# Edge counts as a product of their own in single pass form, and split operands in the first product of an expert layer

## The chip, the cores and the metric

The kernel runs on one core of a Trainium2 chip. The metric is the device time of one execution in microseconds. A core has TensorE (matrix products), VectorE, ScalarE, GpSimd and SyncE, each with its own instruction stream in order, and DMA engines that move data between memories. Engines wait for each other on semaphores. fp32 products are issued as two instructions each; the type fp32r (R32 in the code) is a rounded form that takes one instruction, and full precision is kept by splitting an operand in an upper part (the rounded value) and a lower part (the rest).

## The reference

Two layers over a graph of 3125 nodes with 256 features and 50,000 edges. What matters here:

```python
# first graph layer: messages of 64 features, 4 heads
exp_scores = exp(scores - max)
sum_exp = segment_sum(exp_scores, dst)
outs = [segment_sum(messages * (exp_scores / sum_exp[dst])[:, hd:hd+1], dst) for hd in range(4)]

# first expert layer, 8 experts, each token to its best 2
logits = xf @ gate_w + gate_b
top2_vals, top2_idx = top_k(softmax(logits), 2)
h = gelu(xf @ W1[e] + b1[e])          # 256 -> 512
y = h @ W2[e] + b2[e]                 # 512 -> 256
out = sum over the two experts of weight * y

# second graph layer: mean over incoming edges
deg = segment_sum(ones, dst)
agg = segment_sum(x[src], dst) / max(deg, 1)
```

The degrees of the nodes, which the second layer divides by, are counted in the first layer's edge sums.

## The kernel before

The program is one long sequence of stages, written engine by engine; all order is by hand.

**The edge sums (stage 3).** The 50,000 edges, sorted by destination, lie in 400 chunks of 128. They are worked off in NCG = 40 passes of 10 chunks, in PR = 5 pairs. The edges of a pair fall in a window of W = 48 nodes. For a pass n:
- VectorE (`one_hots`, L3018) writes for each edge the one-hot of its destination in the window, in column block MH = 4 of `ohx`.
- GpSimd (`weigh_hots`, L1052) multiplies it by the exponentials of heads 0 to 2 in two instructions, then sets a column of ones behind the messages (`ones_column`, L1038) and, in the first 25 passes, adds a tile of the input to z (L1063). ScalarE (L2178) does head 3 in ten small instructions.
- TensorE (L1556) multiplies the messages with the column of ones (65 rows) by the five blocks of 48: 240 columns, fp32, two products for each pair. The block of the unweighted one-hots gives the counts in its last row.
- VectorE (`add_windows`, L3034) adds each window of 65 x 5 x 48 at its place in `acc`; each addition waits for the one before.

`ohx` and the messages have two buffers; VectorE issues the one-hots of pass n+1 ahead of the additions of pass n.

**The first expert layer.** The tokens, sorted by expert, form NUN = 32 units of 256 tokens, each with one expert. For a unit u:
- GpSimd fetches its rows of x (L1095), TensorE turns them (`x_turn`, L1631), VectorE copies them from PSUM to `xtT` (`x_keep`, L3260).
- SyncE loads the expert's W1 (512 KB) into one of three buffers of `e1` (`up_weights`, L871). The load of unit u+3 is issued behind the two stores of unit u (L879), which wait for its results.
- For each of MT = 4 blocks f of 128 hidden features: TensorE makes `expert_up(u, f)` (L1642, fp32, 256 columns, two products), ScalarE the gelu (L2211), TensorE `expert_down(u, f)` (L1653, fp32). TensorE issues up of the next step ahead of down of this one, and x_turn(u+2) at f = 2.
- VectorE adds the bias (`keep_y`, L3272) and SyncE stores. VectorE's order in the loop is keep_y(u-1), x_keep(u+2), and at u = 8 to 14 a piece of preparation for the next layer (L3279 to L3291 and the splits at L2594, L2595). In the first turn of SyncE's loop 26 small and large loads for the next layer are issued behind the load of unit 3 (L863).

`hi_lo_products` (L631) makes a product of split operands from three fp32r instructions: upper by upper, upper by lower, lower by upper. It is used in most other stages.

Of the kernel before, what the change touches and what calls it, by code (L numbers as in the profile page):

```python
# [18 lines left out]
F32 = mybir.dt.float32  # L19
R32 = mybir.dt.float32r  # L20
# [5 lines left out]
P = 128  # L26
# [18 lines left out]
W = 48  # L45
# [113 lines left out]
def build(nc, ctx, a, out):  # L159
# [140 lines left out]
    msg = sb("msg", [P, 2, CG, MW], F32, s3)  # L300
    ohx = sb("ohx", [P, 2, CG, MH + 1, W], F32, s3)
    ohs = sb("ohs", [P, WS], F32, s3)
# [66 lines left out]
    hn2 = sb("hn2", [TP, GT, D], F32, s6m)  # L369
    xtT = sb("xtT", [P, 2, H, UT], F32, s6m)  # L370
    be6 = sb("be6", [P, NE, D], F32, s6m)
# [21 lines left out]
    oha = sb("oha", [TP, 2, 2, GT, 2 * NUN], R32, s6m)  # L393
    cc = sb("cc", [TP, NT, NE], F32, s6m)
    s6m.close()
    s6 = ExitStack()
# [35 lines left out]
    aw = sb("aw", [P, H, D], F32, s7k)  # L432
    awx = [sb(f"awx{k}", [P, H, D], R32, s7k) for k in range(2)]
    s7k.close()
    kv = sb("kv", [TP, GT * 2 * H, P + 4], F32, s7)
# [5 lines left out]
    s7k = ExitStack()  # L441
    kvq = sb("kvq", [TP, GT, 2, D], F32, s7k)
    s7k.close()
    mw = [sb(f"mw{k}", [P, 2 * H, D], R32, s7) for k in range(2)]
# [145 lines left out]
    for new, old, value in (("e_ld0", "wq_ld", 128), ("e_ld1", "bo_ld", 128), ("e_ld2", "wvo_ld", 128), ("e_ld3", "sm_ld", 320),  # L590
                            ("row2_st0", "row_st", 32 * NG + 16), ("row2_st1", "x_ld", 32), ("x_ld1", "p7_ld", 0), ("x_ld2", "p9_ld", 0),
                            ("x_ld3", "f_ld0", 0), ("x_ld4", "f_ld1", 0), ("be6_ld", "w_ld", 48),
                            ("z_add", "tn_T", NL), ("z_ve", "cx_ps", NL), ("z_nr", "cx_go", NL), ("hot_w", "bq_ps", NL), ("b1_go", "bq_ev", NL),
                            ("tab_go", "tn_go", NL), ("acc1_0", "ta_go", NL), ("xg_ld0", "gat0", 16 * GC * NCG), ("xg_ld1", "gat1", 16 * GC * NCG),
                            ("xg_T", "n_T", 3 * NG * NL), ("xg_up", "n_hi", 3 * NG * NL),
                            ("yo_go", "m_add", 3 * NG * NL), ("uw_ld0", "msg_st0", 16 * NCG), ("uw_ld1", "msg_st1", 16 * NCG), ("uw_ld2", "msg_ld0", 8 * NCG), ("yo_st0", "w1_ld", 48), ("yo_st1", "w2_ld", 64),
                            ("rw5", "gat0", 16 * GC * NCG + 16 * NUN), ("rw6", "gat1", 16 * GC * NCG + 16 * NUN), ("ch_used", "bc_ps", NL * NG),
                            ("cg_ld0", "rw0", 0), ("cg_ld1", "rw1", 0), ("cg_ld2", "rw2", 0), ("cg_ld3", "rw3", 0),
                            ("cg_used", "d_add", GT * NL * NG), ("tr_hi", "q_hi", 3 * NG * NL)):
        s[new], past[new] = s[old], value  # L600
# [110 lines left out]
    def _(sp):  # L711
# [155 lines left out]
        def up_weights(u):  # L867

            if u >= 3:
                sp.wait_ge(s["up_ps"], F_MOE + (u - 2) * MT)  # L870
            sp.dma_start(e1[:, u % 3, :, :], a["L0_ffn_W1"][expert_of(experts, u)].rearrange("o (h p) n -> p (o h) n", p=P)  # L871
                         ).then_inc(s[f"uw_ld{u % 3}"], 16)
# [64 lines left out]
    def _(pool):  # L937
# [106 lines left out]
        def weigh_hots(n):  # L1044

            if n == 0:
                pool.wait_ge(s["act_go"], 1 + MH)
            pool.wait_ge(s["oh_ready"], n + 1)
            for at in (slice(0, 4), slice(4, CG)):
                cols = slice(n * CG + at.start, n * CG + at.stop)  # L1050
                k = at.stop - at.start
                nc.gpsimd.tensor_tensor(ohx[:, n % 2, at, 0:MH - 1, :], ohx[:, n % 2, at, MH:MH + 1, :].to_broadcast([P, k, MH - 1, W]),  # L1052
                                        ex[:, cols, 0:MH - 1].unsqueeze(3).to_broadcast([P, k, MH - 1, W]),
                                        ALU.mult).then_inc(s["wm_ready"], 1)

        for n in range(NCG):
            weigh_hots(n)
            if n >= 2:
                ones_column(n)
            if n == 0:  # L1060
                pool.wait_ge(s["xin_ld"], 32)
            if n < NT:
                me(nc.gpsimd.tensor_tensor(z[:, n, :], z[:, n, :], xin[:, n, :], ALU.add))  # L1063
        me(nc.gpsimd.memset(tri[:, :, :], 1.0))
# [104 lines left out]
    def _(pe):  # L1169
# [377 lines left out]
        for n in range(NCG):  # L1547
            b = n % 2
            pe.wait_ge(s["msg_one"], n + 1)
            for q in range(PR):  # L1550
                pe.wait_ge(s["wm_ready"], 2 * n + (1 if q < 2 else 2))
                pe.wait_ge(s["ax_ready"], n * PR + q + 1)
                if n:
                    pe.wait_ge(s["win_used"], (n - 1) * PR + q + 1)
                for c in (2 * q, 2 * q + 1):
                    last = nc.tensor.matmul(wbank[q][0:MF + 1, 0:(MH + 1) * W], msg[:, b, c, 0:MF + 1],  # L1556
                                            ohx[:, b, c].rearrange("p k w -> p (k w)"), start=c == 2 * q, stop=c == 2 * q + 1)
                last.then_inc(s["win_ps"], 1)
# [76 lines left out]
        def expert_up(u, f):  # L1635

            F = F_MOE + u * MT + f
            pe.wait_ge(s["xg_up"], past["xg_up"] + u + 1)
            pe.wait_ge(s[f"uw_ld{u % 3}"], past[f"uw_ld{u % 3}"] + 16 * (u // 3 + 1))
            pe.wait_ge(s["gf_done"], F + 1)  # L1640
            for k in range(H):
                last = nc.tensor.matmul(pb[:, f % 2, 0:UT],  # L1642
                                        e1[:, u % 3, k, f * P:(f + 1) * P], xtT[:, u % 2, k, :], start=k == 0, stop=k == H - 1)
            last.then_inc(s["up_ps"], 1)
# [301 lines left out]
    def _(act):  # L1946
# [226 lines left out]
        for n in range(NCG):  # L2173
            b = n % 2
            act.wait_ge(s["oh_ready"], n + 1)
            for q in range(PR):
                for c in (2 * q, 2 * q + 1):
                    last = nc.scalar.mul(ohx[:, b, c, MH - 1, :], ohx[:, b, c, MH, :], ex[:, n * CG + c, MH - 1:MH])  # L2178
                last.then_inc(s["ax_ready"], 1)
# [19 lines left out]
        for g in range(NG):  # L2199
            act.wait_ge(s["dve_go"], 9 + RR + g)  # L2200
            for j in range(GT):
                nc.scalar.mul(oha[:, g % 2, :, j, :], oha[:, g % 2, :, j, :].bitcast(F32), idf[:, g * GT + j:g * GT + j + 1]).then_inc(s["hot_w"], 1)
        nc.scalar.activation(hid[:, 0, 0:1], ones[:, 0:1], ACT.Gelu).then_inc(s["act_go"], 1)
        act.wait_ge(s["act_go"], ACT_GO + 1)
        act.wait_ge(s["b1_go"], past["b1_go"] + 1)
        for u in range(NUN):
            for f in range(MT):
                F = F_MOE + u * MT + f
                act.wait_ge(s["up_ps"], F + 1)
                act.wait_ge(s["act_used"], F + 1)  # L2210
                nc.scalar.activation(hid[:, f, :], pb[:, f % 2, 0:UT], ACT.Gelu, bias=b1u[:, u, f:f + 1]).then_inc(s["gf_done"], 1)  # L2211
        act.nop().then_inc(s["f_hi"], NUN * MT)
        act.wait_ge(s["yo_go"], past["yo_go"] + 2 * NUN)
# [165 lines left out]
    def _(dve):  # L2379
# [636 lines left out]
        def one_hots(n):  # L3016

            nc.vector.tensor_tensor(ohx[:, n % 2, :, MH, :], iota[:, 0:W].unsqueeze(1).to_broadcast([P, CG, W]),  # L3018
                                    relT[:, n * CG:(n + 1) * CG].unsqueeze(2).to_broadcast([P, CG, W]),
# [8 lines left out]
        def add_windows(n, starts):  # L3028

            for q, at in enumerate(starts):  # L3030
                dve.wait_ge(s["win_ps"], n * PR + q + 1)
                if n * PR + q:
                    dve.wait_ge(s["win_used"], n * PR + q)
                nc.vector.tensor_tensor(acc[:, :, bass.ds(at, W)], acc[:, :, bass.ds(at, W)],  # L3034
                                        wbank[q][0:MF + 1, 0:(MH + 1) * W].rearrange("p (k n) -> p k n", k=MH + 1),
                                        ALU.add).then_inc(s["win_used"], 1)

        one_hots(0)
        for n in range(NCG):
# [6 lines left out]
            add_windows(n, window_starts(n))  # L3046
        dve.wait_ge(s["win_used"], NPR)
        dve.wait_ge(s["act_go"], 2 + MH)
        dve.nop().then_inc(s["win_used"], PR)
# [196 lines left out]
        dve.wait_ge(s["tab_go"], past["tab_go"] + 1)  # L3246
        nc.vector.tensor_copy(tabi[:, :], pg[:, 0, 0:2 * NUN]).then_inc(s["tab_go"], 1)
        for f in range(MT):
            me.link(dve, nc.vector.tensor_tensor(hits, own, b1r[:, :, f].unsqueeze(1).to_broadcast(by_unit), ALU.mult))
# [5 lines left out]
        def x_keep(u):  # L3255

            dve.wait_ge(s["xg_T"], past["xg_T"] + u + 1)
            if u >= 2:
                dve.wait_ge(s["up_ps"], F_MOE + (u - 1) * MT)
            nc.vector.tensor_copy(xtT[:, u % 2], pt[:, u % 2, :].rearrange("p (k n) -> p k n", k=H)).then_inc(s["xg_up"], 1)  # L3260

# [36 lines left out]

        x_keep(0)
        x_keep(1)  # L3300
        dve.wait_ge(s["pe_go"], 12 + RR)
# [3 lines left out]
        for u in range(NUN):  # L3305
            if u:
                keep_y(u - 1)
            if u + 2 < NUN:
                x_keep(u + 2)
            if u == 8:  # L3310
# [401 lines left out]
```

## Time and profile before

| | us |
|---|---|
| median of 3 runs | 2693.89 (2690.0 to 2704.63) |
| the profiled execution | 2691.82 |
| its span in the trace | 2690.1 |
| edge sums | about 1259 to 1443 |
| loop over the expert units | 1541.5 to 1779.2 |

In rows that list instructions in order of time the columns are: start, duration, engine, line, operation, output <- input, shapes, count, and in brackets how long the engine had been idle and what ended that. PE is TensorE, PEld its weight loads, DVE VectorE, ACT ScalarE, POOL GpSimd, SPq the queue of SyncE. The granted clock of TensorE is given as a share of 2.4 GHz.

### The profile page before, as it was taken

How to read it: one execution, taken by the hardware profiler on the slowest of the kernel's cores; microseconds unless marked ns; L12 is line 12 of the kernel's file. 1: busy time of each engine (PE TensorE's matmuls, PEld its weight loads, DVE VectorE, ACT ScalarE, POOL GpSimd, SP SyncE). 2: the span in 40 equal slices, each digit the busy share in tenths (PEclk: the TensorE clock that was granted, in tenths of full speed). 3: DMA queues.
4: the chain of work that ended last, by engine and by line, in shares of the span. 5: the costliest groups of instructions: out<-in, count | busy, mean ns of one | idle time of the engine just before them, and what ended most of it. 6: DMA issues, size and time to landing. Idle time of an engine off the chain costs nothing. (4 is left out here: it accounts for less than half of the span.)

```text
span 2690.1 us, 46341 instructions
## 1 busy us (share of the span) xinstructions
PE 2428.9 (90%) x16026; PEld 2242.4 (83%) x16026; DVE 1738.7 (65%) x4274; ACT 1352.7 (50%) x2913; POOL 1244.5 (46%) x1402
## 2 busy tenths in 40 slices
PE   6888999899989998997999699966888999999998
PEld 6778998899988997996668688855778799998998
DVE  6666877678767776764656523246876677677565
ACT  4334656466545655555553322233234366665687
POOL 1323454245524551564876232245767377776000
PEclk9789999999999999999997599977989699999899
DMA  5211112111121111124223354536666076775011
GB/s 119 67 39 40 40 43 76 32 40 43 43 66 38 44 46 48 45 58 101 79 84 91 106 169 144 144 111 179 199 194 193 17 215 200 219 220 177 24 36 32
DMA packets 150284, 259.75 MB, mean 97 GB/s; under 512 B 35713, under 2 KB 95884, under 8 KB 149926
## 3 DMA queue, kind: packets, MB, share of 16 engines
q0 software_dynamic: 49632, 145.61, 19.9%
q1 hardware_dynamic: 100422, 111.17, 13.7%
q8 instruction: 132, 2.16, 0.3%
q14 instruction: 98, 0.80, 0.1%
HBM read 219.88 MB, written 36.82 MB: 95 GB/s over the span
## 5 line engine op out<-in xcount | busy, mean ns | idle before, releaser
L974 POOL DMA_INDIRECT gat<-table,srcT x400 | 414.2, 1036 | 352.9 <-DVE m L2820 230.3
L1129 POOL DMA_INDIRECT x_rows<-table,srcT x392 | 402.2, 1026 | 176.9 <-issue 122.7
L631 PE MATMUL pa<-w,act 128*125 128x256 f32 x2400 | 359.2, 288 | 13.0 <-DVE act L2579 12.8
L631 PE MATMUL pb<-hT,w 128*128 128x378 f32 (+1 forms) x1920 | 337.2, 312 | 1.8 <-DVE hT L2655 1.0
L631 PEld LDWEIGHTS pa<-w,act 128*125 128x125 f32 x2400 | 314.6, 187 | 17.7 <-DVE act L2579 17.6
L631 PEld LDWEIGHTS pb<-hT,w 128*128 128x128 f32 x1920 | 287.7, 190 | 4.1 <-DVE hT L2655 1.8
L2278 ACT ACTIVATE gf<-pb,bne 128x378 f32<-128x378 f32 (+1 forms) x320 | 193.9, 606 | 154.9 <-PE pb L631 143.5
L2579 DVE TENSOR_TENSOR act<-gf,act 128x378 fp32r<-128x378 f32 (+1 forms) x320 | 153.8, 483 | 106.7 <-ACT act L1996 104.9
L1993 ACT ACTIVATE gf<-pb,b1s 128x378 f32<-128x378 f32 (+1 forms) x320 | 165.6, 517 | 108.2 <-PE pb L631 98.3
L631 PE MATMUL pb<-xT,fw 128*128 128x378 f32 (+1 forms) x960 | 158.8, 316 | 0.0
L1996 ACT ACTIVATE act<-gf 128x378 fp32r<-128x378 f32 (+1 forms) x320 | 149.8, 468 | 10.1
L2211 ACT ACTIVATE hid<-pb,b1u 128x256 f32<-128x256 f32 x128 | 60.6, 473 | 185.0 <-PE pb L1642 185.0
L631 PE MATMUL pb<-act,fw 128*128 128x378 f32 (+1 forms) x960 | 153.4, 309 | 0.0
L3555 DVE TENSOR_TENSOR act<-gf,act 128x378 fp32r<-128x378 f32 (+1 forms) x180 | 87.8, 488 | 101.3 <-ACT act L2282 100.6
L1095 POOL DMA_INDIRECT xtok<-table,tabi x64 | 61.4, 959 | 190.2 <-PE pt L1631 139.7
L631 PEld LDWEIGHTS pb<-xT,fw 128*128 128x128 f32 x960 | 146.1, 196 | 1.4 <-issue 1.3
L631 PEld LDWEIGHTS pb<-act,fw 128*128 128x128 f32 x960 | 141.7, 190 | 0.0
L2178 ACT ACTIVATE ohx<-ohx,ex 128x48 f32<-128x48 f32 x400 | 94.4, 321 | 84.3 <-DVE ohx L3018 84.3
L1642 PE MATMUL pb<-xtT,e 128*128 128x256 f32 x512 | 132.9, 382 | 2.3 <-DVE xtT L3260 2.3
L1730 PE MATMUL pg<-x_rows,oh 128*125 128x256 f32 x632 | 105.1, 294 | 27.4 <-DMA x_rows<-table,srcT 17.8
L1052 POOL TENSOR_TENSOR ohx<-ohx,ex 128x576 f32<-128x576 f32 x80 | 110.0, 1396 | 35.5 <-DVE ohx L3018 35.2
L1556 PE MATMUL pa<-ohx,msg 128*65 128x240 f32 x480 | 106.5, 372 | 15.7 <-POOL ohx L1052 12.6
(513 smaller groups left out, 5602.5 us busy)
## 6 DMA issues: line engine op xcount, KB each, us to landing
e<-in_L_ffn_W_dram SPq DMA_DIRECT2D x40, 512.0 KB, 4.1
spill<-m SPq DMA_DIRECT2D x80, 170.0 KB, 1.9
msg<-spill SPq DMA_DIRECT2D x40, 340.0 KB, 2.9
yslots<-yo SPq DMA_DIRECT2D x64, 128.0 KB, 2.0
fraw<-in_L_ffn_W_dram SPq DMA_DIRECT2D x32, 256.0 KB
w1r<-in_L_mix_W_dram SPq DMA_DIRECT2D x7, 1024.0 KB, 5.0
gat<-table,srcT POOLq DMA_INDIRECT x400
x_rows<-table,srcT POOLq DMA_INDIRECT x392, 3.7
```

What stands on the lines that cost most here:

```text
L631: mm = nc.tensor.matmul(ps, lhs(l), rhs(r), start=first and n == 0, stop=last and n == 2)
L974: pool.indirect_dma_start(out=gat[:, i % 2, c, :], out_offset=None, in_=table0, in_offset=bass.IndirectOffsetOnAxis(ap=srcT[:, i * GC + c: ...
L1052: nc.gpsimd.tensor_tensor(ohx[:, n % 2, at, 0:MH - 1, :], ohx[:, n % 2, at, MH:MH + 1, :].to_broadcast([P, k, MH - 1, W]), ex[:, cols, 0:M ...
L1129: pool.indirect_dma_start(out=x_rows[:, n % UB, c, :].bitcast(F32), out_offset=None, in_=table1, in_offset=bass.IndirectOffsetOnAxis(ap=sr ...
L1556: last = nc.tensor.matmul(wbank[q][0:MF + 1, 0:(MH + 1) * W], msg[:, b, c, 0:MF + 1], ohx[:, b, c].rearrange("p k w -> p (k w)"), start=c ...
L1642: last = nc.tensor.matmul(pb[:, f % 2, 0:UT], e1[:, u % 3, k, f * P:(f + 1) * P], xtT[:, u % 2, k, :], start=k == 0, stop=k == H - 1)
L1730: last = nc.tensor.matmul(to, oh1[:, n % UB, c, :], x_rows[:, n % UB, c, k * D:(k + 1) * D], start=c == 0 and k == 0, stop=c == UG - 1 and ...
L1993: nc.scalar.activation(gf[:, f % 2, 0:n], pb[:, f % 2, 0:n], func, bias=bias, scale=scale).then_inc(s["gf_done"], 1)
L1996: nc.scalar.activation(act_[0][:, f % 4, 0:n], gf[:, f % 2, 0:n], ACT.Copy).then_inc(s["f_hi"], 1)
L2178: last = nc.scalar.mul(ohx[:, b, c, MH - 1, :], ohx[:, b, c, MH, :], ex[:, n * CG + c, MH - 1:MH])
L2278: nc.scalar.activation(gf[:, f % 2, 0:n], pb[:, f % 2, 0:n], func, bias=bias, scale=scale).then_inc(s["gf_done"], 1)
L2579: nc.vector.tensor_tensor(act_[1][:, f % 4, 0:n], gf[:, f % 2, 0:n], act_[0][:, f % 4, 0:n], ALU.subtract).then_inc(s["f_lo"], 1)
```

## The change

The edge sums: the one-hots get a tile of their own, `ohd`, in fp32r. The five blocks of `ohx` become four. The counts are made by two fp32r products a pass (the even and the odd chunks of all five pairs, 240 columns) of a tile of ones by the one-hots, into a PSUM bank of their own, and VectorE adds them to `acc` in an addition of 48 columns behind each window's. The additions of GpSimd to z are spread over the 40 passes.

The expert layer: W1 of a unit is split into `e1s[0]` (ScalarE, `up_upper`, behind the gelu of the same f two units ahead) and `e1s[1]` (VectorE, `up_lower`, behind keep_y(u-1) and ahead of x_keep(u+2)); `xtT` is split by x_keep in two operations. `expert_up` uses hi_lo_products. The loads of e1 wait for the lower parts in place of the products. `expert_down` stays as it is.

```diff
-    ohx = sb("ohx", [P, 2, CG, MH + 1, W], F32, s3)
+    ohx = sb("ohx", [P, 2, CG, MH, W], F32, s3)
+    ohd = sb("ohd", [P, 2, CG, W], R32, s3)
+    ohd_one = sb("ohd_one", [P, MF + 1], R32, s3)
...
         def up_weights(u):
             if u >= 3:
-                sp.wait_ge(s["up_ps"], F_MOE + (u - 2) * MT)
+                sp.wait_ge(s["us_lo"], past["us_lo"] + (u - 2) * MT)
...
-            if n < NT:
-                me(nc.gpsimd.tensor_tensor(z[:, n, :], z[:, n, :], xin[:, n, :], ALU.add))
+            for t in range(n * NT // NCG, (n + 1) * NT // NCG):
+                me(nc.gpsimd.tensor_tensor(z[:, t, :], z[:, t, :], xin[:, t, :], ALU.add))
...
+                if q == 0:
+                    if n >= 2:
+                        pe.wait_ge(s["deg_used"], past["deg_used"] + (n - 1) * PR)
+                    hots = ohd[:, b].rearrange("p (q k) w -> p q k w", k=2)
+                    for k in range(2):
+                        nc.tensor.matmul(pt[0:MF + 1, b, 0:PR * W].rearrange("p (q w) -> p q w", q=PR), ohd_one[:, :], hots[:, :, k, :],
+                                         start=k == 0, stop=k == 1)
                 for c in (2 * q, 2 * q + 1):
-                    last = nc.tensor.matmul(wbank[q][0:MF + 1, 0:(MH + 1) * W], msg[:, b, c, 0:MF + 1],
+                    last = nc.tensor.matmul(wbank[q][0:MF + 1, 0:MH * W], msg[:, b, c, 0:MF + 1],
...
         def expert_up(u, f):
-            pe.wait_ge(s[f"uw_ld{u % 3}"], past[f"uw_ld{u % 3}"] + 16 * (u // 3 + 1))
+            pe.wait_ge(s["us_lo"], past["us_lo"] + u * MT + f + 1)
             for k in range(H):
-                last = nc.tensor.matmul(pb[:, f % 2, 0:UT],
-                                        e1[:, u % 3, k, f * P:(f + 1) * P], xtT[:, u % 2, k, :], start=k == 0, stop=k == H - 1)
+                last = hi_lo_products(pb[:, f % 2, 0:UT], lambda l: e1s[l][:, u % 2, k, f * P:(f + 1) * P],
+                                      lambda r: xtT[r][:, u % 2, k, :], k == 0, k == H - 1)
...
+        def up_upper(u, f):
+            if f == 0:
+                act.wait_ge(s[f"uw_ld{u % 3}"], past[f"uw_ld{u % 3}"] + 16 * (u // 3 + 1))
+            at = slice(f * P, (f + 1) * P)
+            nc.scalar.activation(e1s[0][:, u % 2, :, at], e1[:, u % 3, :, at], ACT.Copy).then_inc(s["us_hi"], 1)
+        for u in range(2):
+            for f in range(MT):
+                up_upper(u, f)
...
                 nc.scalar.activation(hid[:, f, :], pb[:, f % 2, 0:UT], ACT.Gelu, bias=b1u[:, u, f:f + 1]).then_inc(s["gf_done"], 1)
+                if u + 2 < NUN:
+                    up_upper(u + 2, f)
...
+                degrees = acc[:, MH:MH + 1, bass.ds(at, W)].rearrange("p o n -> p (o n)")
+                nc.vector.tensor_tensor(degrees, degrees, pt[0:MF + 1, n % 2, q * W:(q + 1) * W], ALU.add).then_inc(s["deg_used"], 1)
...
+        def up_lower(u, f):
+            dve.wait_ge(s["us_hi"], past["us_hi"] + u * MT + f + 1)
+            at = slice(f * P, (f + 1) * P)
+            nc.vector.tensor_tensor(e1s[1][:, u % 2, :, at], e1[:, u % 3, :, at], e1s[0][:, u % 2, :, at], ALU.subtract).then_inc(s["us_lo"], 1)
+        for f in range(MT):
+            up_lower(0, f)
...
-            nc.vector.tensor_copy(xtT[:, u % 2], pt[:, u % 2, :].rearrange("p (k n) -> p k n", k=H)).then_inc(s["xg_up"], 1)
+            turned = pt[:, u % 2, :].rearrange("p (k n) -> p k n", k=H)
+            me.link(dve, nc.vector.tensor_copy(xtT[0][:, u % 2], turned))
+            nc.vector.tensor_tensor(xtT[1][:, u % 2], turned, xtT[0][:, u % 2], ALU.subtract).then_inc(s["xg_up"], 1)
...
         x_keep(0)
+        for f in range(MT):
+            up_lower(1, f)
         x_keep(1)
...
             if u:
                 keep_y(u - 1)
             if u + 2 < NUN:
+                for f in range(MT):
+                    up_lower(u + 2, f)
                 x_keep(u + 2)
```

## Rows read from the trace of the kernel before

**Rows 1.** The page, part 1: busy time, share of the span, instructions
```profile
PE 2428.9 (90%) x16026; PEld 2242.4 (83%) x16026; DVE 1738.7 (65%) x4274; ACT 1352.7 (50%) x2913; POOL 1244.5 (46%) x1402
```

**Rows 2.** Stretch of the expert loop: busy time by engine, clock, DMA
```profile
1541.50:1779.20 237.70, 236.93 (x1150) 207.79 (x1150) 56.73 (x119) 60.59 (x128) 61.59 (x60) 0.99 0.47 142
```

**Rows 3.** Waits in the expert loop: total us, times, longest
```profile
ACT hid L2211 <- PE pb L1642: 173.8, 127, 2.7
```

**Rows 4.** Order of time, end of one expert unit, all engines
```profile
1661.59 1.03 PE L1642 MATMUL pb<-xtT,e 128*128 128x256 f32 x4
...
1662.45 0.59 PE L1653 MATMUL pa<-e,hid 128*128 x2
1662.65 0.47 ACT L2211 ACTIVATE hid<-pb,b1u 128x256 f32<-128x256 f32 x1 [1.69 <-PE pb L1642]
...
1663.19 0.42 DVE L3272 TENSOR_TENSOR yo<-pa,be 128x256 f32<-128x256 f32 x1 [1.58 <-PE pa L1653]
1663.31 1.03 PE L1642 MATMUL pb<-xtT,e 128*128 128x256 f32 x4
1663.62 0.42 DVE L3272 TENSOR_TENSOR yo<-pg,be 128x256 f32<-128x256 f32 x1
...
1664.62 0.39 SPq L871 DMA_DIRECT2D e<-in_L_ffn_W_dram  x1
```

**Rows 5.** Order of time, two passes of the edge sums
```profile
1327.18 2.65 PE L1556 MATMUL pa<-ohx,msg 128*65 128x240 f32 x12
1327.34 0.40 DVE L3034 TENSOR_TENSOR acc<-acc,pb 65x240 f32 x1 [0.41 <-PE pb L1556]
1327.66 0.65 DVE L3018 TENSOR_TENSOR ohx<-iota,relT 128x480 f32<-128x480 f32 x1
...
1328.39 2.75 POOL L1052 TENSOR_TENSOR ohx<-ohx,ex 128x576 f32<-128x576 f32 x2 [0.60 <-DVE ohx L3018]
...
1329.66 1.78 PE L1556 MATMUL pb<-ohx,msg 128*65 128x240 f32 x8
...
1331.28 2.61 PE L1556 MATMUL pa<-ohx,msg 128*65 128x240 f32 x12
...
1335.49 2.65 PE L1556 MATMUL pa<-ohx,msg 128*65 128x240 f32 x12
```

**Rows 6.** Order of time in another stage: fp32r products, a copy by ScalarE
```profile
1241.25 0.88 PE L631 MATMUL pa<-w,act 128*125 128x256 f32 x6
...
1241.95 0.41 ACT L1996 ACTIVATE act<-gf 128x252 fp32r<-128x252 f32 x1
1241.97 0.86 PE L631 MATMUL pb<-hT,w 128*128 128x252 f32 x6
```

**Rows 7.** VectorE's groups in the expert loop: busy us, mean ns, idle before
```profile
L2595 DVE TENSOR_TENSOR kvw<-qw,kvw 128x256 fp32r<-128x256 f32 x4 | 1.7, 424 | 0.1
...
L3280 DVE TENSOR_SCALAR kvm<-kvm 125x16 f32<-125x16 f32 x1 | 0.2, 181 | 0.0
```

**Rows 8.** Single lines of VectorE: ns min/median/max, first and last start
```profile
L3260 DVE COPY xtT<-pt x32: 681/691/692, 1540.8 to 1763.8; 128x512 f32<-128x512 f32 x32
...
L3290 DVE TENSOR_TENSOR qw<-qw,wmean x2: 691/692/692, 1618.4 to 1625.9; 128x512 f32<-128x512 f32 x2
```

**Rows 9.** The loads of e1 (L871, 32 of them), from issue to landing
```profile
DMA to landing us min/median/max: 3.6/3.9/6.5
```

**Rows 10.** TensorE behind two gaps, and the clock behind the first
```profile
1868.74 0.76 PE L1730 MATMUL pg<-x_rows,oh 128*125 128x256 f32 x2 [4.92 <-DMA x_rows<-table,srcT]
1870.09 0.79 PE L1730 MATMUL pg<-x_rows,oh 128*125 128x256 f32 x2 [0.58 <-DMA x_rows<-table,srcT]
...
1249.40 1.69 PE L631 MATMUL pa<-w,act 128*125 128x256 f32 x12 [3.02 <-DVE act L2579]
...
1868.74:1873.38 4.64, 2.92 (x8) 2.04 (x9) 0.00 (x0) 0.00 (x0) 3.42 (x5) 0.50 0.70 210
```

**Rows 11.** SyncE's queue: the loads of e1 for units 3 and 4
```profile
1553.48 0.39 SPq L871 DMA_DIRECT2D e<-in_L_ffn_W_dram  x1
...
1568.15 0.40 SPq L871 DMA_DIRECT2D e<-in_L_ffn_W_dram  x1
```

More of the change, by code:

```diff
@@ L369, in build @@
     hn2 = sb("hn2", [TP, GT, D], F32, s6m)
-    xtT = sb("xtT", [P, 2, H, UT], F32, s6m)
+    xtT = [sb("xtT", [P, 2, H, UT], R32, s6m)]
     be6 = sb("be6", [P, NE, D], F32, s6m)
@@ L394, in build @@
     cc = sb("cc", [TP, NT, NE], F32, s6m)
+    e1s = [sb("e1s0", [P, 2, H, MT * P], R32, s6m)]
     s6m.close()
@@ L433, in build @@
     awx = [sb(f"awx{k}", [P, H, D], R32, s7k) for k in range(2)]
+    xtT.append(sb("xtT1", [P, 2, H, UT], R32, s7k))
     s7k.close()
@@ L442, in build @@
     kvq = sb("kvq", [TP, GT, 2, D], F32, s7k)
+    s7k.close()
+    s7k = ExitStack()
+    e1s.append(sb("e1s1", [P, 2, H, MT * P], R32, s7k))
     s7k.close()
@@ L592, in build @@
                             ("x_ld3", "f_ld0", 0), ("x_ld4", "f_ld1", 0), ("be6_ld", "w_ld", 48),
-                            ("z_add", "tn_T", NL), ("z_ve", "cx_ps", NL), ("z_nr", "cx_go", NL), ("hot_w", "bq_ps", NL), ("b1_go", "bq_ev", NL),
+                            ("z_add", "tn_T", NL), ("z_ve", "cx_ps", NL), ("z_nr", "cx_go", NL), ("hot_w", "bq_ps", NL), ("b1_go", "bq_ev", NL), ("deg_used", "mo_ps", NL), ("us_hi", "bq_go", NL), ("us_lo", "km_go", NL * NG),
                             ("tab_go", "tn_go", NL), ("acc1_0", "ta_go", NL), ("xg_ld0", "gat0", 16 * GC * NCG), ("xg_ld1", "gat1", 16 * GC * NCG),
@@ L1051, in weigh_hots @@
                 k = at.stop - at.start
-                nc.gpsimd.tensor_tensor(ohx[:, n % 2, at, 0:MH - 1, :], ohx[:, n % 2, at, MH:MH + 1, :].to_broadcast([P, k, MH - 1, W]),
+                nc.gpsimd.tensor_tensor(ohx[:, n % 2, at, 0:MH - 1, :], ohd[:, n % 2, at, :].bitcast(F32).unsqueeze(2).to_broadcast([P, k, MH - 1, W]),
                                         ex[:, cols, 0:MH - 1].unsqueeze(3).to_broadcast([P, k, MH - 1, W]),
@@ L2177, in _ @@
                 for c in (2 * q, 2 * q + 1):
-                    last = nc.scalar.mul(ohx[:, b, c, MH - 1, :], ohx[:, b, c, MH, :], ex[:, n * CG + c, MH - 1:MH])
+                    last = nc.scalar.mul(ohx[:, b, c, MH - 1, :], ohd[:, b, c, :].bitcast(F32), ex[:, n * CG + c, MH - 1:MH])
                 last.then_inc(s["ax_ready"], 1)
@@ L3016, in one_hots @@
         def one_hots(n):
-            nc.vector.tensor_tensor(ohx[:, n % 2, :, MH, :], iota[:, 0:W].unsqueeze(1).to_broadcast([P, CG, W]),
+            nc.vector.tensor_tensor(ohd[:, n % 2], iota[:, 0:W].unsqueeze(1).to_broadcast([P, CG, W]),
                                     relT[:, n * CG:(n + 1) * CG].unsqueeze(2).to_broadcast([P, CG, W]),
@@ L3033, in add_windows @@
                     dve.wait_ge(s["win_used"], n * PR + q)
-                nc.vector.tensor_tensor(acc[:, :, bass.ds(at, W)], acc[:, :, bass.ds(at, W)],
-                                        wbank[q][0:MF + 1, 0:(MH + 1) * W].rearrange("p (k n) -> p k n", k=MH + 1),
+                nc.vector.tensor_tensor(acc[:, 0:MH, bass.ds(at, W)], acc[:, 0:MH, bass.ds(at, W)],
+                                        wbank[q][0:MF + 1, 0:MH * W].rearrange("p (k n) -> p k n", k=MH),
                                         ALU.add).then_inc(s["win_used"], 1)
+                if n * PR + q:
+                    dve.wait_ge(s["deg_used"], past["deg_used"] + n * PR + q)
+                degrees = acc[:, MH:MH + 1, bass.ds(at, W)].rearrange("p o n -> p (o n)")
+                nc.vector.tensor_tensor(degrees, degrees, pt[0:MF + 1, n % 2, q * W:(q + 1) * W], ALU.add).then_inc(s["deg_used"], 1)
+        me.link(dve, nc.vector.tensor_copy(ohd_one[:, :], ones[:, 0:MF + 1]))
         one_hots(0)
@@ L3047, in _ @@
         dve.wait_ge(s["win_used"], NPR)
+        dve.wait_ge(s["deg_used"], past["deg_used"] + NPR)
         dve.wait_ge(s["act_go"], 2 + MH)
```

## Prediction, made before the changed kernel was built

> **What bounds the kernel now.** I read the page's engine totals first: TensorE is busy 90% of the span, the next engine 65% [rows 1]. That is a mean over stages, so the stretches of the two edited stages come next.
>
> In the expert loop (L1642, L1653) TensorE is busy 236.9 of 237.7 us at a granted clock of 0.99 [rows 2], and ScalarE waits for it 127 times, 173.8 us in all [rows 3]. TensorE alone sets the pace. Its fp32 products are two instructions each. One f step is four for "up" and four for "down", 0.86 us each (1661.59 to 1662.45 to 1663.31) [rows 4]: 0.215 us for an instruction of 256 columns. Four transposes of 128 columns add half of that each, 0.43 us (estimate). A unit is 4 x 1.72 + 0.43 = 7.3 us, and 32 of them are the 237.7 us.
>
> The edge sums look TensorE bound too, but the order of time shows a second limit. A pass of 20 instructions starts at 1327.18; the next but one at 1335.49, so 4.155 us a pass [rows 5]. TensorE itself needs 2.48 us for 12 instructions (to 1329.66), so about 4.05 for 20. What closes the gap is a chain over two passes: last product of a pass, last window's addition (1327.34), the next one-hots (1327.66), GpSimd's weighting (1328.39, 2.75 us), the ones column, then the pass at 1331.28. From the end of the issue of one pass to the start of the pass after next that is about 4.28 us: 2 x 4.155 = 4.03 + 4.28. TensorE's pass is only half of what sets the period.
>
> **Part 1, counts in single pass form.** The rhs of 800 instructions shrinks from 240 to 192 columns: 20 x 0.2 x 0.8 = 3.2 us a pass. Two fp32r products of 240 columns come in. In fp32r, six instructions of 256 or 252 columns follow each other in 0.70 to 0.72 us (1241.25 to 1241.97) [rows 6], so 0.12 each. A pass becomes 3.4 us. VectorE's addition of 240 columns (0.40) [rows 5] loses 48 columns, about 0.05, and gets a small one beside it. No row has 48 columns from PSUM: between 0.18 (16 columns) [rows 7] and 0.40 (240 columns); I take 0.2, near the small end. Most of it fills time in which an addition waits anyway for the one before, as both touch the same accumulator. On the two-pass chain one small addition is added, some 0.1 us: 4.38. The new period is (3.4 + 4.38)/2 = 3.89, a gain of 0.27 x 40, so **10 us**. Bounds: if VectorE, with five instructions more a pass, becomes the limit, the period stays near 4.15 and the gain is 0 (at 0.4 for each of them, 2 us a pass, even a loss is possible: 0.2 a pass, 8 us); with the small addition free it is 12. GpSimd's residual additions are only spread over the passes and come after the ones column, off the chain: nothing. The new wait of TensorE at q = 0 is for additions two passes old: nothing.
>
> **Part 2, products.** An up step goes from four instructions of 0.215 to six of 0.12: 0.71 for 0.86. 128 x 0.15 = 19 us less on TensorE, 6.7 us a unit. That would be the gain if TensorE still set the pace.
>
> **Part 2, what feeds them.** Each f step now needs a ScalarE copy of 128x256 (0.41 for 252 columns) [rows 6], a VectorE subtraction (0.42) [rows 7], and each unit a second 128x512 operation from PSUM behind the first (0.69 and 0.69) [rows 8]. By total there is room: 4 x (0.47 + 0.41) on ScalarE in 6.7 us. What matters is where the copies stand. up_upper(u+2, 0) is issued behind gelu(u, 0), and it waits for the load of unit u+2. SyncE issues that load behind the stores of unit u-1, whose bias additions follow down(u-1, 3). But gelu(u, 0) runs while down(u-1, 3) is still being issued: ScalarE at 1662.65, the additions at 1663.19 and 1663.62, the load's issue at 1664.62 [rows 4]. It lands 3.9 us after (3.6 at least) [rows 9], so near 1668.5. Today nobody needs it for two more units. After the change ScalarE is stopped by it from 1663.1, and all gelus of unit u stand behind it on the same in-order engine. TensorE can do up 1, down 0 and up 2, then it stops too.
>
> So the loop becomes a ring through the load. From one landing to the next:
> - copy 0.41, gelu 0.47: 0.88
> - down(u,1) 0.86 and up(u,3) 0.71: 2.45
> - drain and start of gelu 3, 0.2, and 0.47: 3.12
> - copy 0.41, subtraction 0.42: 3.95
> - the two 128x512 operations of x_keep, 0.69 each: 5.33. Keep_y of this unit stands behind them on VectorE; down(u,3) has then its first half, at about 5.2
> - second bias addition 0.43 later, load's issue 1.00 after that (1663.62 to 1664.62): 6.76
> - landing 3.9: **10.7 us** for 7.3 now.
>
> **Clock.** In this ring TensorE stands still about 4 us a period. After 4.92 us of idle time its pairs took 0.79 us and the granted clock was 0.50, the lower level of 1.2 GHz, for the next 4.6 us; after 3.02 us of idle time twelve instructions took 1.69 us, the quick pace [rows 10]. Four us lies between. If the level is low, the down and up behind the landing take 1.57 us more: 12.3. If it stayed low for the whole period, the way over x_turn, down 2, up 0 and half of down 3 would be the longer one: about 14.5 (twice 4.0 on TensorE, with 0.88, 0.2 and 5.3 of the rest). I take 11.8, low after two gaps in three. The Trainium skill ("TensorE: Matmul & The Clock Gate", HAM oscillation) describes a loop in which each wait for a transfer throws the array back to its low rate, so that each burst starts cold. By that rule every period would be 12.3, 13 us more in the sum; the two gaps quoted leave it open for 4 us.
>
> The same skill ("DMA: Bandwidth & Descriptors", Rules for kernel authors) wants a transfer issued early and waited for late; the change moves the wait from two units after the issue to right behind it, and the 3.9 us of the row is then on the path.
>
> **Sum for the loop.** The loop starts at 1541.5. VectorE first makes four subtractions (1.7) and the second 0.69: 2.4 us later. The load of unit 3, issued at 1553.48 now [rows 11], comes 2.5 later (2.4 + 0.7 for the order of keep_y, less 0.6), 1556.0. The load of unit 4 comes 14.7 us behind it, since SyncE issues 26 other loads between them (1553.48 to 1568.15) [rows 11]: 1570.7, landed 1574.6. Then 27 periods to the load of unit 31: 27 x 11.8 = 318.6. VectorE's preparation for the next layer (11 groups, 9.7 us busy, the costliest and the least in [rows 7]) stands between x_keep and keep_y, today in idle time, then on the ring: 9.3 after overlap. From the last landing (in unit 29) to the end: 6.5 for the rest of 29, 6.3 and 5.6 for units 30 and 31, 18.9 with some clock loss. End: 1574.6 + 318.6 + 9.3 + 18.9 = 1921.4, for 1779.3: **142 us more**.
>
> Against the profiled execution's own 2691.8 us (span 2690.1): 2691.8 + 142 - 10 = 2824. The median shown is 2 us above that execution, which changes nothing here.
>
> **Rivals.**
> (a) The ring at full clock: 10.7 a period, 30 us less, 2794. For it: 3.02 us of idle time left the clock high.
> (b) The ring at the low clock throughout: 14.5 a period, 73 us more, 2897. For it: 4.6 us at 0.50 behind one gap, though with TensorE less busy than here.
> (c) Not slower: the gain of the title. If ScalarE weren't held by the load (it would have to land within 0.5 us of the end of down 3, where 3.6 is the least seen), TensorE keeps the pace: 2691.8 - 19 - 10 + 2 = 2665. It decides at a landing before the next gelu is due, which the order of issue forbids; only a misreading of that order leaves it a chance.
> (d) Part 1 gives nothing because VectorE limits the pass: 2834. It moves the forecast inside its range only.
>
> **How the numbers follow.** Chances: ring with a mixed clock 0.50, (a) 0.24, (b) 0.18, (c) 0.06, something near no change 0.02. The likeliest gives 2824. The range runs from (a) with a landing of 3.6 (27 x 0.3 = 8 less), 2786, to (b), 2897; (c) and what lies beyond those ends is left out. About 0.5% (13 us) is what a measurement of this kernel can tell from no change: slower 0.93, same 0.02, faster 0.05.
>
> **What would show it.** Right: ScalarE's copies at the new up_upper line wait for the DMA of e some 28 times, 3 to 5 us each; load issues in the loop 11 to 12 us apart; TensorE busy near 60 to 70% of the loop and a granted clock well under 0.99; the last down product near 1920 less the gain ahead; edge passes 3.9 us apart. Wrong: load issues 6.7 us apart with TensorE full; or a ring that is closed by another wait than the load; or copies much longer than 0.41 us.

## The result: 2846 us, 5.6% slower

The changed kernel takes 2846.08 us (median; 2843.96 to 2855.87), the kernel before 2694.39: a ratio of 1.056 (95% interval 1.0537 to 1.0582), 152 us more. The forecast was 2824. The profiled execution took 2846.21 us with a span of 2844.3.

The page's engine totals answer to [rows 1]:

```profile
PE 2462.9 (87%) x16362; PEld 2306.7 (81%) x16362; DVE 1831.2 (64%) x4635; ACT 1389.7 (49%) x3041; POOL 1243.6 (44%) x1402
```

TensorE is less busy by share and yet busy for 34 us more in all, although its work is shorter at the full clock (0.71 us for 0.86 in an up step, by the prediction's rows): the first sign of a lower clock. Where the time went is seen in the stretch of the expert loop, up to its last product (1928.3 us now, 1779.3 before), beside [rows 2]; the columns are the same:

```profile
1541.50:1928.50 387.00, 271.59 (x1373) 243.73 (x1372) 123.71 (x266) 91.77 (x242) 59.06 (x57) 0.81 0.29 86
```

TensorE was busy all the time there; now it is idle for 115 of 387 us, and the granted clock is 0.81 for 0.99. The waits of the changed kernel between 1500 and 1960 us, which takes in the loop (total us, times, longest), answer to [rows 3]:

```profile
DVE e1s L3285 <- ACT e1s L2224: 236.9, 117, 6.3
ACT e1s L2224 <- DMA e<-in_L_ffn_W_dram: 165.0, 29, 6.8
ACT hid L2236 <- PE pb L638: 142.2, 70, 10.5
...
PE pa L1667 <- ACT hid L2236: 115.2, 29, 5.1
```

The new wait is the second row: ScalarE's first copy of a unit (L2224 is up_upper) waits for the load of W1, 29 times, 165 us. The gelus stand behind it, and TensorE's down product (L1667) behind them: 29 times, 115.2 us, which is all of its idle time.

The chain that ended last, in order of time, shows one whole turn of the ring at the full clock (start, duration, what; the short steps left out are hand-overs of 0.02 to 0.13 us, among them the start of ScalarE's copy at 1751.81):

```profile
1748.40 3.38 DMA e<-in_L_ffn_W_dram
...
1752.13 0.47 ACT hid L2236
...
1752.72 0.69 PE pa L1667 x2
1753.42 0.43 PE pg L1667 x2
1753.85 0.70 PE pb L638 x6
1754.56 0.44 PE pt L1645 x4
...
1755.86 0.71 PE pb L638 x6
1756.56 0.45 PE pa L1667 x2
...
1757.14 0.41 DVE yo L3315
...
1757.64 0.44 DVE yo L3315
1758.09 0.32 SPq L886
...
1758.59 4.33 DMA e<-in_L_ffn_W_dram
```

From the issue of one load to the issue of the next are 10.19 us: 3.4 until the load has landed and ScalarE starts, and 6.8 from there. The same stretch, issue to issue, for one period at the full clock and one at a low one (columns as in the expert loop's row above):

```profile
1598.07:1608.25 10.18, 7.00 (x45) 6.38 (x45) 3.83 (x8) 3.01 (x8) 1.89 (x2) 1.00 0.32 105
1798.06:1811.78 13.72, 9.74 (x45) 8.61 (x45) 3.85 (x8) 3.01 (x8) 1.91 (x2) 0.75 0.27 79
```

The same instructions in both, 3.5 us apart. Of the 27 periods between the issues of the loads of units 4 and 31, four had a granted clock of 1.00 (10.2 to 10.4 us), sixteen 0.74 to 0.76 (13.0 to 13.9) and seven one between (11.8 to 13.8). Their mean is 12.75.

The edge sums gained as forecast. In the order of time, TensorE's count products open the passes at 1321.54, 1325.61 and 1329.35: 3.9 us a pass, for 4.155 in [rows 5].

```profile
1321.54 0.44 PE L1567 MATMUL pt<-ohd,ohd_one 128*65 128x240 f32 x2 [0.38 <-POOL msg L1045]
...
1325.37 0.35 DVE L3061 TENSOR_TENSOR acc<-acc,pb 65x192 f32 x1 [0.18 <-PE pb L1570]
...
1325.61 0.43 PE L1567 MATMUL pt<-ohd,ohd_one 128*65 128x240 f32 x2 [0.38 <-POOL msg L1045]
1325.64 0.19 DVE L3067 TENSOR_TENSOR acc<-acc,pt 65x48 f32 x1
1325.76 0.65 DVE L3045 TENSOR_TENSOR ohd<-iota,relT 128x480 fp32r<-128x480 f32 x1
1325.88 2.11 PE L1570 MATMUL pa<-ohx,msg 128*65 128x192 f32 x12
...
1329.35 0.43 PE L1567 MATMUL pt<-ohd,ohd_one 128*65 128x240 f32 x2
```

### The profile page after: what moved, and what is told of

Read it like the earlier page. It is cut to its first block and busy times, and to the rows that moved or that the text cites. A ratio compares the mean times of both kernels' runs of the same rounds, so it can differ in the third digit from the quotient of the medians.

```text
span 2844.3 us, 47704 instructions
## 1 busy us (share of the span) xinstructions
PE 2462.9 (87%) x16362; PEld 2306.7 (81%) x16362; DVE 1831.2 (64%) x4635; ACT 1389.7 (49%) x3041; POOL 1243.6 (44%) x1402
## 3 DMA queue, kind: packets, MB, share of 16 engines
q1 hardware_dynamic: 100422, 111.17, 13.2%
## 5 line engine op out<-in xcount | busy, mean ns | idle before, releaser
L1667 PE MATMUL pa<-e,hid 128*128 x384 | 131.9, 460 | 115.2 <-ACT hid L2236 115.2
L3285 DVE TENSOR_TENSOR e1s<-e,e1s 128x256 fp32r<-128x256 f32 x128 | 53.7, 425 | 236.9 <-ACT e1s L2224 236.9
L1667 PEld LDWEIGHTS pa<-e,hid 128*128 128x128 f32 x384 | 77.5, 232 | 126.8 <-issue 121.1
L638 PE MATMUL pb<-xtT,e1s 128*128 128x256 f32 x768 | 157.4, 347 | 4.0 <-DVE xtT L3303 4.0
L2010 ACT ACTIVATE act<-gf 128x378 fp32r<-128x378 f32 (+1 forms) x320 | 149.8, 468 | 10.2
L638 PEld LDWEIGHTS pb<-xtT,e1s 128*128 128x128 f32 x768 | 128.6, 221 | 14.9 <-DVE xtT L3303 4.3
```

Source lines behind the costliest of these rows:

```text
L638: mm = nc.tensor.matmul(ps, lhs(l), rhs(r), start=first and n == 0, stop=last and n == 2)
L1667: mm = nc.tensor.matmul(y_banks[u % 2][i][:, 0:D], hid[:, f, i * P:(i + 1) * P], e2[:, expert_of(experts, u), f, :].rearrange("p o d -> p ...
L2010: nc.scalar.activation(act_[0][:, f % 4, 0:n], gf[:, f % 2, 0:n], ACT.Copy).then_inc(s["f_hi"], 1)
L3285: nc.vector.tensor_tensor(e1s[1][:, u % 2, :, at], e1[:, u % 3, :, at], e1s[0][:, u % 2, :, at], ALU.subtract).then_inc(s["us_lo"], 1)
```

## The experiments

Theory: the expert loop runs as a ring through the load of W1, which is issued too late for the copy that waits for it, and each turn is longer where TensorE's clock is low. Rivals: the copies and subtractions cost the time by their own length or by contention; the edge sums have a part in it; the clock is a bystander; VectorE's preparation for the next layer throws the loop off.

The kernels e1 to e4 were measured beside the kernel before at 2695.0, e9 and e10 at 2692.4. Those of e5 to e8 were measured later, when the same kernel before took 2835.5, some 140 us more; why is not known, so they are compared with that time, by ratio or difference. The loop's own length seems not to be touched by it (the expert layer of e6 and e9 is the same, and its loop takes 218.2 and 218.7 us). It is given from the start of the first gelu to the start of the last, which is 234.0 us in the kernel before and 390.4 in the changed one, each in one profiled execution.

**e1, the counts alone.** The kernel before with the change in the edge sums only.

> The kernel before with the counts of edges alone changed; the expert layer as before. Theory (the two-pass chain of the edge sums): passes about 3.9 us apart for 4.155, a gain of 10 us, 2684. Rival (VectorE's five additions more a pass take the gain): passes stay at 4.15, 2694 or up to 2702. If the parts act on each other by the clock, this one and the next do not add up to the whole.

Measured: 2686.8 for 2695.0, ratio 0.9966 (0.995 to 0.9982), 8 us gained by the medians and 9 by the ratio; the loop is 232.6 us. The passes open at 1312.80, 1316.53, 1320.67, 1324.73 and 1328.47, 3.92 apart. TensorE is no longer full (92.5 of 100 us, 1300 to 1400) and waits for the ones column, the last step of the chain over two passes: the chain is what is left, as the prediction had it.

```profile
POOL ohx L1054 <- DVE ohd L3027: 27.2, 35, 1.9
PEld pt L1562 <- POOL msg L1040: 22.4, 34, 1.2
```

**e2, the expert layer alone.**

> The kernel before with the expert layer alone changed. Theory (the ring through the load of W1): the loss of the whole change and the 10 us that the counts gain, 2856; ScalarE's copies wait 29 times for the load, load issues 10.2 us apart at the full clock and 13 to 14 at the low one. Rival (the loss comes from both parts, for instance from the edge sums' later clock or bank use): clearly under 2846.

Measured: 2853.08, ratio 1.06 (1.0565 to 1.0636); the loop is 389.7 us. ScalarE's wait for the load is there again, a little longer:

```profile
  DMA e<-in_L_ffn_W_dram: 169.7, 29
```

The parts add up: 1.06 times 0.9966 is 1.056. The whole loss is in the expert layer.

**e3, the load ahead of the stores.** One exchange in SyncE's order:

```diff
         for u in range(NUN):
+            if u + 3 < NUN:
+                up_weights(u + 3)
             for i in range(2):
                 sp.wait_ge(s["yo_go"], past["yo_go"] + 2 * u + i + 1)
                 sp.dma_start(yslots[(2 * u + i) * P:(2 * u + i + 1) * P, :], yo[:, i, :]).then_inc(s[f"yo_st{i}"], 16)
-            if u + 3 < NUN:
-                up_weights(u + 3)
```

> The changed kernel; SyncE issues the load of unit u+3 ahead of the stores of unit u in place of behind them, nothing else. Theory (ring): the load no longer hangs on the results of unit u, lands before it is wanted, and TensorE sets the pace again at 6.7 us a unit; one wait of about 10 us stays at unit 4, whose load stands behind the 26 other loads: 2694 - 10 - 19 + 2 + 10 = 2677. Rival (the copies and subtractions themselves, by their time on ScalarE and VectorE or by contention for the memory, cost the 152 us): hardly changed, above 2800.

Measured: 2680.95, ratio 0.9956 (0.9941 to 0.9972). The loop falls from 390.4 to 227.7 us, and from 1600 to 1700 TensorE has no rest:

```profile
1600.00:1700.00 100.00, 100.00 (x656) 93.77 (x655) 63.18 (x142) 46.59 (x119) 27.62 (x30) 1.00 0.52 157
```

From the load of unit 6 on, the load issues are 5.9 to 7.0 us apart, but for one of 8.5. Ahead of that, where the 26 other loads are issued, stand one gap of 13.0 and TensorE's one wait for a gelu, of 11.4 us. All copies, subtractions and products of the change are still made. So it isn't their work that costs the time; it is the order of one issue. This is the experiment that decides.

**e4, the gap filled.** Products that feed nothing, where TensorE would stand still:

```diff
+            if f == 1 and 1 <= u < NUN - 2:
+                for _ in range(14):
+                    nc.tensor.matmul(pt[:, u % 2, 0:P], ones[:, :], ones[:, :], start=True, stop=True)
             expert_down(u, f)
```

> The changed kernel with 14 products of 128 columns of ones more for TensorE in units 1 to 29, ahead of down 1, where it otherwise stands still; they feed nothing. Theory (the clock is some 2.5 us of each period of 12.75): it stays at the full clock, periods of 10.2 to 10.5 and 9 us for VectorE's preparation, 2788, though TensorE does more. Rival (the low clock only goes along with a ring whose length is set by the load and the other engines): no gain, 2846 or more by the 3 us a unit of the added products, up to 2930.

Measured: 2816.05, ratio 1.0444 (1.041 to 1.0478): 30 us better than the changed kernel with 812 instructions more. Both expectations missed; it lies between. The granted clock of the loop is 0.97:

```profile
1536.00:1899.00 363.00, 323.28 (x2214) 302.88 (x2212) 126.22 (x270) 93.98 (x248) 60.52 (x59) 0.97 0.32 92
```

So the clock is a cause, not a bystander, and it is lost through the rests: in the 27 periods between the issues of the loads of units 4 and 31, what lies behind the landings adds up to 203.7 us for 236.7. The landings took 113.7 for 107.5 and gave part of it back. But the periods are not the 10.2 to 10.5 expected; two of them:

```profile
1797.21:1807.63 10.42, 10.11 (x73) 9.52 (x73) 3.83 (x8) 3.00 (x8) 1.89 (x2) 1.00 0.31 98
1807.63:1819.61 11.98, 10.13 (x73) 9.54 (x73) 3.83 (x8) 3.00 (x8) 1.90 (x2) 1.00 0.30 88
```

The same clock, the same work, 1.56 us apart. The rest is the landing. ScalarE's first copies of these periods and the load issues before them:

```profile
1797.21 0.39 SPq L878 DMA_DIRECT2D e<-in_L_ffn_W_dram  x1
1807.63 0.39 SPq L878 DMA_DIRECT2D e<-in_L_ffn_W_dram  x1
...
1800.86 0.42 ACT L2227 ACTIVATE e1s<-e 128x256 fp32r<-128x256 f32 x1 [5.15 <-DMA e<-in_L_ffn_W_dram]
1812.82 0.42 ACT L2227 ACTIVATE e1s<-e 128x256 fp32r<-128x256 f32 x1 [6.69 <-DMA e<-in_L_ffn_W_dram]
```

3.65 us and 5.19 us from issue to copy; taken off, 6.77 and 6.79 are left. In 17 of the 27 periods, all at the full clock, a period is 6.8 us plus the landing. The other ten are those of units 8 to 14, with VectorE's preparation, two at a lowered clock, and one in which SyncE took 2.80 us for the two stores in place of 0.80.

**e5, the copies one unit ahead.** ScalarE's and VectorE's work is moved to one unit before its use in place of two; SyncE's order is the changed kernel's.

```diff
-                if u + 2 < NUN:
-                    up_upper(u + 2, f)
+                if u + 1 < NUN:
+                    up_upper(u + 1, f)
...
-            if u + 2 < NUN:
+            if u + 1 < NUN:
                 for f in range(MT):
-                    up_lower(u + 2, f)
+                    up_lower(u + 1, f)
+            if u + 2 < NUN:
                 x_keep(u + 2)
```

> The changed kernel; behind gelu(u, f) ScalarE copies the block of unit u+1 in place of unit u+2, and VectorE's subtractions move with it; SyncE's order as in the changed kernel. Theory (ring): the same copies, with a load issued one unit earlier than it is wanted; TensorE sets the pace at 6.7 us, with one wait of about 4 us for the load of unit 4: 2694 - 10 - 19 + 2 + 4 = 2671, under the 2681 of the kernel with the loads first. Rival (the copies hinder by where they stand between the gelus, now with less slack to their use): above 2681.

Measured: ratio 0.9932 (0.9906 to 0.9957), less than the kernel before beside it by 23.7 us in the medians and 19 by the ratio; the loop is 222.7 us. Expected were 23 us under before. It mends the same fault from the other end: the copy asks for a load that was issued a unit earlier. With less slack between copy and use it is no slower.

**e6, both, and the load of unit 4 early.** e3 and e5 together, and the load of unit 4 ahead of the 26 loads for the next layer.

> The two remedies together (loads ahead of the stores, copies one unit ahead), and the load of unit 4 issued ahead of the 26 loads for the next layer. Theory: no wait for a load is left in the loop; 2694 - 10 - 19 + 2 = 2667. If 2671 or more, something else than the load of unit 4 holds the start of the loop.

Measured: ratio 0.9901 (0.9873 to 0.9929), 28 us less than the kernel before beside it; the loop is 218.2 us, and ScalarE has no wait for a load in it. From before's 2694.4 that ratio is 2668. This kernel is faster than the kernel before and the changed one; its 4 us against e5 are not clear of the noise.

**e7, the gap filled further**, with 18 products for 14.

> The kernel with the gap filled, with 18 products more for 14, which end about when the load lands (0.45 to 2.4 us of idle time were left, and the clock still fell in some periods). Theory (what was left of the clock's share is due to those rests): periods of 10.3 to 10.6, 27 x 1.3 = 35 us under the 2816 of 14 products, 2781 to 2790. Rival (the clock's share was the 30 us and the rest of the periods is longer landings): 2816 or somewhat more by the four added products.

Measured: ratio 1.0389 (1.0359 to 1.0418), the loop 362.1 us for 361.0 in e4: no gain in the loop, against the theory, which wanted 35 us. The whole is 111 us above the kernel before beside it, where e4 was 121 above its own; the intervals of the two ratios overlap. The clock was at 1.00 in 26 of the 27 periods now. But the shortest is 10.74, since four products more end later than a quick load lands, and the slow landings (4.5 us and more in 14 of the 27) stay. So 14 products had won nearly all of the clock's share; for the loop the rival had it right.

**e8, VectorE's preparation behind the loop.** centre_bias, centre_weights and the splits are taken out of units 8 to 14 and follow the last keep_y.

> The changed kernel; VectorE's preparation for the next layer stands behind the loop in place of units 8 to 14. Theory as in the prediction (it lies on the ring, 9.3 us): those are saved in the loop and up to 9.7 come back behind it, 2837 to 2847. Rival A (at the low clock TensorE's way is longer and hides it): the loop saves under 3 us, 2846 to 2855. Rival B (it is what throws the loop out of the periods of 10.2 us that stood before unit 8 into those of 13): the loop keeps its 10.2 and saves up to 20 x 3 = 60 us, near 2796.

Measured: ratio 1.049 (1.0462 to 1.0519), the loop 375.1 us for 390.4. Fifteen us saved in the loop are more than the first two expectations and far fewer than rival B's. Nine of the 27 periods had a granted clock of 1.00, for four in the changed kernel, so the 15 us can't be divided between the preparation's own time and the clock. The loop kept its short period in unit 8 (10.38) and left it in unit 9 (12.70, with a landing of 4.3 us) though no preparation was there; in the changed kernel it left it in unit 8, with the preparation and a landing of 4.4. So a late landing is enough, and rival B is not the whole of it. Nor is it nothing: in e2 the loads of units 10 and 11 landed quickly, in 3.5 and 3.7 us, and the loop left its short period there all the same. The periods of units 8 and 9 of e2:

```profile
1637.46:1649.39 11.93, 8.12 (x52) 7.25 (x51) 5.22 (x11) 3.01 (x8) 1.90 (x2) 1.00 0.30 97
1649.39:1663.07 13.68, 8.43 (x44) 7.54 (x44) 5.41 (x12) 3.01 (x8) 1.90 (x2) 0.88 0.25 76
```

In the first, 8.5 us lie between landing and issue for the 6.8 of a period without the preparation, and TensorE's next rest is 5.2 us. Either can lengthen the rest, a late landing or the preparation. What the preparation costs on the ring is seen at the full clock in e4: periods less landing of 8.6, 9.0 and 8.3 us at units 9, 10 and 12, for 6.8 in the 17 periods named there. In the changed kernel, at the low clock, units 9 and 10 had 10.1 and 10.4, units 11 to 14 8.9 to 9.6, and the periods without preparation 8.6 to 9.7: there it is mostly hidden.

**e9, the expert layer alone with the remedies of e6.**

> The expert layer's change alone, with loads ahead of the stores, copies one unit ahead and the load of unit 4 early; the edge sums as before. Theory (with TensorE at full rate the six fp32r products for four fp32 instructions are worth 19 us, 2 come back at the start): ratio to before 0.9937, 17 us. Rival (the gain of the last kernels is mostly the edge sums' and the time of the products is not won): under 10 us, ratio above 0.996.

Measured: 2678.76 for 2692.39, ratio 0.9941 (0.9919 to 0.9963), 16 us by the ratio (10 to 22) and 14 by the medians, for 17 expected; the loop is 218.7 us for 234.0. The split product is worth what its instruction counts say once nothing waits.

**e10, the load behind the first half of the results.** SyncE issues it before both stores, as soon as the first of the two bias additions is done.

```diff
                 sp.wait_ge(s["yo_go"], past["yo_go"] + 2 * u + i + 1)
+                if i == 0 and u + 3 < NUN:
+                    up_weights(u + 3)
                 sp.dma_start(yslots[(2 * u + i) * P:(2 * u + i + 1) * P, :], yo[:, i, :]).then_inc(s[f"yo_st{i}"], 16)
-            if u + 3 < NUN:
-                up_weights(u + 3)
```

> The changed kernel; SyncE issues the load as soon as the first half of the unit's results is there, ahead of both stores. Theory (every step from the landing to the issue is on the ring): the second bias addition and the two stores' issue, some 0.9 us, fall out of each period, 9.3 at the full clock, so 24 us less than the changed kernel's, and up to 50 if the shorter rest keeps the clock up more often: ratio to before 1.037 to 1.048 for 1.056. Rival (the ring is closed by something else, for instance by TensorE at the low clock, or the stores and the load only change places in the queues): 1.055 or more.

Measured: 2823.82, ratio 1.0476 (1.0452 to 1.05), 22 us better than the changed kernel, at the near end of the range expected; in the profiled executions the loop is 375.9 us for 390.4. But not as expected: at the full clock the periods stayed at 10.1 to 10.5.

```profile
1588.42 0.94 SPq L888 DMA_DIRECT2D yslots<-yo  x2
...
1592.49 0.42 ACT L2224 ACTIVATE e1s<-e 128x256 fp32r<-128x256 f32 x1 [5.18 <-DMA e<-in_L_ffn_W_dram]
...
1597.21 0.95 POOL L1102 DMA_INDIRECT xtok<-table,tabi  x1 [0.30 <-issue]
...
1598.43 0.39 SPq L878 DMA_DIRECT2D e<-in_L_ffn_W_dram  x1
```

The load issued at 1587.98 is used at 1592.49, 4.5 us later, where quick ones took 3.4 to 3.6 in the changed kernel. The part behind the landing fell from 6.8 to 5.9, as worked out, and the landing took it back. The gain came where the clock is lowered: 12.2 to 13.2 for 13.0 to 13.9 in units 8 to 14, and over all 27 periods 11 at 0.73 to 0.76 for 16. So the range was met, and not for the reason it was given for.

## Why the prediction was right

**What bounds the loop, and the ring.** Right. The reading on which the forecast rested was one of order: gelu(u, 0) is due while down(u-1, 3) is issued, and the load that the new copy asks for is issued behind the results of that same unit [rows 4]. e3 and e5 take that wait away from either end and bring the loop to 228 and 223 us. One sum on the way is loose: 32 units of 7.3 us are 234 us, which is the loop from its first gelu to its last, and not the whole stretch of 237.7.

**The steps of the ring.** 6.76 us from landing to issue were worked out from single durations; 6.8 is measured. The two ways of the sum (VectorE's over x_keep, TensorE's over down 3) are in fact within 0.1 us of each other: in the turn shown, the chain goes over TensorE. The landing was 3.9 by [rows 9]; it is 3.4 to 5.1 in the 27 periods, 4.0 on the mean.

**The start.** Load of unit 3: forecast at 1556.0 less the 10 us of the edge sums, 1546.0; measured 1546.13. Load of unit 4: 1560.7; measured 1560.15.

**The clock.** The mechanism is right, its size is the term that was too small. I took a clock that is low behind two gaps in three and recovers after down 1 and up 3, 11.8 us a period. Measured are 13.0 to 13.9 in sixteen of 27 periods at a granted clock of 0.75: TensorE's way stays slow beyond those two products, and 8.6 to 10.4 us lie behind the landing for 6.8. With the preparation my 27 periods come to 318.6 + 9.3 = 327.9 us; they took 344.2, 16 us more: 2 in the landings and 14 behind them. The Trainium skill's picture of a loop that is thrown back to the low rate by each wait for a transfer ("TensorE: Matmul & The Clock Gate", HAM oscillation) is what most periods show (23 of 27 below 1.00), and I gave it too little; the four periods at 1.00, with 3.2 to 3.4 us of rest before the down product, show that it isn't a rule for this gap. e4 prices it: 30 us for the whole kernel, later landings included.

**The preparation.** 9.3 us were put on the ring. At the full clock it is there (1.5 to 2.2 us in each of units 9, 10 and 12 of e4), at the low clock mostly not, so in this kernel that term was too large, and the clock's error still larger. The two errors have opposite signs, and that the forecast came within 22 us is in part owed to that; how much each is worth was not separated.

**The landing on the path.** The rule cited from the Trainium skill ("DMA: Bandwidth & Descriptors", Rules for kernel authors: issue early, wait late) is borne out: with the same copies the loop is 163 us shorter when the load is issued ahead of the stores (e3).

**The counts.** Forecast 10 us and passes of 3.89; measured 8 to 9 us and 3.9. The prediction puts TensorE's 20 instructions at 4.05 us; by its own row (2.48 for 12) they take 4.13, which would move the forecast period by 0.02. The small addition takes 0.19 us (taken: 0.2). The bound with a loss through VectorE didn't come up.

**The rest.** From the last product of the loop to the end of the span there are 916.0 us now and 910.8 before; 5 of the 22 us missing are there. In e1 it is 911, in e3 908. TensorE is busy 9 us more in that part with the same work, and the granted clock is 0.68 for 0.72 in its first 121 us and 0.87 for 0.89 in another stretch; why the clock differs there was not followed up.

**The rivals.** (c), the gain of the title, needed a load that lands in time; e3, e5 and e6 give it that and come to 2668 to 2681, where the forecast for (c) was 2665. (a) and (b) bracket the result.

**The signs.** ScalarE's copies wait 29 times for the load, as forecast (28), but 5.7 us on the mean and up to 6.8, for 3 to 5: the wait also holds the time in which ScalarE would have stood idle before the load was issued. The load issues are 10.2 to 13.9 us apart, 12.75 on the mean, for 11 to 12. TensorE is busy 70% of the loop, at the end of the range of 60 to 70%, and the last down product comes at 1928.3 for some 1910.

## What to carry to other kernels

When work is moved ahead of its use, its input must be there ahead too: look not at how long the load takes but at which instruction it is issued behind, and compare the two times in one unit of the trace. A wait on an in-order engine stops everything behind it, here the gelus. Here the load ahead of the stores turns 5.6% slower into 0.4% faster, a lookahead of one unit instead of two into 0.7%, and both, with the load of unit 4 early, into 1.0%. And where a wait for a transfer leaves TensorE idle for a few microseconds in each turn of a loop, price the turn at the low clock too.

## What the runs showed of the hardware that I had not expected

- The rest alone does not tell the clock. With the same instructions, the changed kernel had periods of 10.2 to 10.4 us at a granted clock of 1.00 (rest of TensorE before down 1: 3.2 to 3.4 us), three of them in a row in units 5 to 7. In unit 18 came a late landing (4.4 us, rest 4.2), and behind it four periods at 0.74 to 0.75 with rests of 3.4 to 4.0. A rest of 3.42 us stands in a period at 1.00 (unit 6), one of 3.41 in a period at 0.74 (unit 19).
- From the issue of a load of 512 KB to the copy that waits for it are 3.4 to 5.1 us in the loop of the changed kernel and 3.3 to 6.7 in e7. In e10, issued 0.9 us closer behind GpSimd's row fetches and ahead of the two stores, it took some 0.8 us longer at the full clock. That it shares the engines with those is likely but was not separated; why most of the loads of units 22 to 30 in e4 take 4.3 to 5.6 us at an unchanged pattern is open.
